# A sequence adapter kernel: another order of the beginning, high by high first

## The reference

```python
h = jnp.einsum('bsh,bhk->bsk', hidden_states, W_down[role]) + b_down[role][:, None, :]   # 1024 -> 512
h = jax.nn.gelu(h, approximate=False)
u = jnp.einsum('bsk,bkh->bsh', h, W_up[role]) + b_up[role][:, None, :]                   # 512 -> 1024
y = hidden_states + u
mean = jnp.mean(y, axis=-1, keepdims=True)
var = jnp.mean(jnp.square(y - mean), axis=-1, keepdims=True)
yn = (y - mean) * jax.lax.rsqrt(var + LN_EPS)
return yn * gamma[role][:, None, :] + beta[role][:, None, :]
```

## Time and profile before

| | us |
|---|---|
| median of 3 runs | 1417.29 (1417.27 to 1417.34) |
| the profiled execution | 1416.96 |
| its span | 1415.2 |
| PE busy | 1401.1 (99%) |
| DVE busy | 1204.8 (85%) |
| ACT busy | 776.8 (55%) |
| GpSimd busy | 201.0 (14%) |
| moved by DMA | 283.49 MB, 200 GB/s in the mean |

### The profile page before, as it was taken

One profiled execution on the slowest core, in us unless ns is written; L12 is line 12 of the kernel. 1 busy time (PEld: TensorE's weight loads), 2 busy tenths in 40 slices (PEclk: granted clock), 3 DMA queues, 4 the chain that ended last, 5 costly groups with the idle time before them and its releaser, 6 DMA issues.

```text
span 1415.2 us, 29331 instructions
## 1 busy us (share of the span) xinstructions
PE 1401.1 (99%) x6175; PEld 1158.2 (82%) x6176; DVE 1204.8 (85%) x1458; ACT 776.8 (55%) x2047; POOL 201.0 (14%) x300
## 2 busy tenths in 40 slices
PE   8999999999999999999999999999999999999997
PEld 6888888888888888888888888888888888888886
DVE  8798988888888888888888899988888888888887
ACT  5555555555555555555555555555555555555555
POOL 4376311100000000000000377311100000000000
PEclk9999999999999999999999999999999999999999
DMA  8677777766566666665666778777765666656654
GB/s 230 183 225 241 215 212 200 211 195 198 184 195 199 194 184 196 200 192 184 194 200 193 213 227 234 222 198 201 218 199 185 196 200 190 185 194 199 192 186 149
DMA packets 208868, 283.49 MB, mean 200 GB/s; under 512 B 25791, under 2 KB 155584, under 8 KB 208846
## 3 DMA queue, kind: packets, MB, share of 16 engines
q1 hardware_dynamic: 201438, 269.34, 61.4%
q0 software_dynamic: 5888, 12.07, 4.6%
q10 hardware_dynamic: 1520, 1.84, 0.4%
HBM read 183.27 MB, written 99.88 MB: 200 GB/s over the span
## 4 chain that ended last, share of the span: by engine, by line
PE 98%; DVE 1%; DMA 1%; issue 0%; ACT 0%; DVEq 0%; ACTq 0%
PE p_up L1120 16%; PE p_up L1118 16%; PE p_up L1119 16%; PE p_down L1118 16%; PE p_down L1120 16%; PE p_down L1119 16%; DMA row<-in_L_cond_W_down 0%; DMA x_quad<-in_x 0%; DVE row L1038 0%; PE p_hT L1114 0%; DVE row L866 0%; DMA w_raw<-in_itok_B 0%; DVE x_quad L820 0%; DVE wd_lo L758 0%; DVE x_quad L1024 0%
## 5 line engine op out<-in xcount | busy, mean ns | idle before, releaser
L1118 PE MATMUL p_down<-wd_hi,xT_hi 128*128 x1012 | 393.9, 389 | 0.7 <-DVE xT_lo L782 0.4
L1120 PE MATMUL p_down<-wd_hi,xT_lo 128*128 x1012 | 393.7, 389 | 0.0
L1119 PE MATMUL p_down<-wd_lo,xT_hi 128*128 x1012 | 393.7, 389 | 0.0
L1118 PE MATMUL p_up<-wu_hi,hT_hi 128*128 x1008 | 392.3, 389 | 0.0
L1120 PE MATMUL p_up<-wu_hi,hT_lo 128*128 x1008 | 392.1, 389 | 0.0
L1119 PE MATMUL p_up<-wu_lo,hT_hi 128*128 x1008 | 392.1, 389 | 0.0
L595 ACT ACTIVATE hT_hi<-p_hT 128x512 fp32r<-128x512 f32 x126 | 75.7, 601 | 381.5 <-DVE p_hT L800 378.9
L820 DVE SCALAR_TENSOR_TENSOR row<-p_up,row 128x1024 f32<-128x1024 f32 x126 | 154.2, 1224 | 126.3 <-PE p_up L1120 126.2
L581 ACT ACTIVATE xT_hi<-xT_raw 128x1024 fp32r<-128x1024 f32 x125 | 132.8, 1062 | 187.6 <-PE p_down L1120 185.6
L1118 PEld LDWEIGHTS p_down<-wd_hi,xT_hi 128*128 128x128 f32 x1012 | 189.6, 187 | 40.8 <-issue 1.4
L1119 PEld LDWEIGHTS p_down<-wd_lo,xT_hi 128*128 128x128 f32 x1012 | 190.3, 188 | 39.7
(11 more groups left out here) (174 smaller groups left out, 981.3 us busy)
## 6 DMA issues: line engine op xcount, KB each, us to landing
x_quad<-in_x SPq DMA_DIRECT2D x510, 128.0 KB, 3.4
row<-in_x SPq DMA_DIRECT2D x126, 512.0 KB, 4.0
out<-row SPq DMA_DIRECT2D x126, 512.0 KB, 2.7
h_dram<-h SPq DMA_DIRECT2D x125, 256.0 KB, 4.1
h_quad<-h_dram SPq DMA_DIRECT2D x498, 64.0 KB, 1.9
w_raw<-in_L_cond_W_down POOLq DMA_DIRECT2D x64, 64.0 KB, 3.2
w_raw<-in_L_cond_W_up POOLq DMA_DIRECT2D x64, 64.0 KB, 3.6
row<-in_L_cond_W_up SPq DMA_DIRECT2D x16, 128.0 KB, 3.6
```

Source lines behind the costliest of these rows:

```text
L1118: pe.matmul(dst, a_hi, w_hi, start=first, stop=False)
L1119: pe.matmul(dst, a_hi, w_lo, start=False, stop=False)
L1120: return pe.matmul(dst, a_lo, w_hi, start=False, stop=last)
```

## The change

- **Loads.** ACT issues only half of piece 1, rounds piece 0 first, and issues its two quarters of the first x after that. SP issues the other half of piece 1 behind its two quarters of the first x, then the second x, then pieces 2 and 3 whole. The numbers are read with one load instead of one for each x.
- **Parameter rows.** Their rounding moves from DVE to ACT, their subtraction behind `split_first(0)`.
- **DVE.** The selector is built ahead of the sort, the identity later. Both halves of the first x are transposed at once; `transpose_half(1, 1)` moves behind `split_first(2)` and `split_first(3)`.
- **ACT.** `round_first(1)` moves behind `round_half(0, 0)`, `copy_param(1)` behind `round_half(0, 1)`.
- **PE.** The matmuls on zeros go (with GpSimd's memset); five on W follow piece 0 and the two later ones go. `half_product` issues, for items 1 and 2, high by high of four chunks, high by low of four, then low by high; for item 0 it goes by pairs of chunks, each kind of matmul behind the wait for what it needs.

The number of product matmuls stays the same. The diff, with one line of context and without the list of semaphores:

```diff
@@ -307,10 +307,13 @@
 
+            number_reg = [sp.alloc_register(f"first_number{n}") for n in range(RING)]
             sp.wait_ge(first_known, 1)
-            for b, quads in ((0, range(0, NQ // 2)), (1, range(NQ))):
-                load_quads(sp, sp.value_load(first_numbers[0:1, b:b + 1], min_val=0, max_val=B - 1), b, quads)
-            load_first(sp, FD - 2, range(NQ // 2, NQ))
+            sp.load(number_reg, first_numbers[0:1, 0:RING])
+            load_quads(sp, sp.snap(number_reg[0], min_val=0, max_val=B - 1), 0, range(0, NQ // 2))
+            load_first(sp, 1, range(NQ // 2, NQ))
+            load_quads(sp, sp.snap(number_reg[1], min_val=0, max_val=B - 1), 1)
+            load_first(sp, FD - 2)
             load_first(sp, FD - 1)
@@ -396,7 +399,6 @@
             pool.memset(opener[:, 0:2], 0.0).then_inc(pieces_split, 1)
-            pool.memset(xT_lo[:, 0:HALF, :].bitcast(F32), 0.0).then_inc(zeros_ready, 1)
 
@@ -468,7 +470,7 @@
-            pool.wait_ge(ident_ready, 1)
+            pool.wait_ge(ident_ready, 2)
@@ -548,14 +550,20 @@
             load_first(act, 0, range(1, NQ))
-            load_first(act, 1)
-            act.wait_ge(first_known, 1)
-            load_quads(act, act.value_load(first_numbers[0:1, 0:1], min_val=0, max_val=B - 1), 0, range(NQ // 2, NQ))
+            load_first(act, 1, range(0, NQ // 2))
 
...
                 act.activation(hi, buf, ACT.Copy).then_inc(first_hi, 1)
+
+            round_first(0)
+            number_reg = [act.alloc_register(f"first_number{n}") for n in range(RING)]
+            act.wait_ge(first_known, 1)
+            act.load(number_reg, first_numbers[0:1, 0:RING])
+            load_quads(act, act.snap(number_reg[0], min_val=0, max_val=B - 1), 0, range(NQ // 2, NQ))
+            act.wait_ge(param_rows_loaded, 16 * 8)
+            act.activation(rows, rows_raw, ACT.Copy).then_inc(param_rows_hi, 1)
 
@@ -671,16 +679,14 @@
 
-            round_first(0)
             act.wait_ge(order_in_psum, 1)
             act.activation(table[0:1, NUMBER:NUMBER + B], p_up[0][0:1, 2 * B:3 * B], ACT.Copy).then_inc(numbers_ready, 1)
+            round_half(0, 0)
             round_first(1)
-            round_half(0, 0)
-            load_first(act, FD - 2, range(0, NQ // 2))
             copy_param(2, p_up[1][:, :], BETA, H, beta_loaded)
-            copy_param(1, p_hT[:, :], BD, K, bias_loaded)
             round_half(1, 0)
             round_half(0, 1)
+            copy_param(1, p_hT[:, :], BD, K, bias_loaded)
             round_first(2)
@@ -739,18 +745,17 @@
 
-            dve.wait_ge(key_spread, 1)
-            chain(dve.tensor_copy(key_col[:, :], p_up[0][:, B:B + 1]))
-            chain(dve.tensor_scalar(onehot, p_up[0][:, 0:B], key_col[:, :], None, ALU.is_gt, ALU.add, accum_out=rank[:, :]))
-            dve.tensor_scalar(onehot, index_row, rank[:, :], None, ALU.is_equal).then_inc(order_ready, 1)
-
             dve.tensor_scalar(row_of_col[:, 0:1].bitcast(I32), index_col[:, :], BLK - 1, None, ALU.bitwise_and).then_inc(row_known, 1)
...
                               ALU.is_equal).then_inc(ident_ready, 1)
-            dve.tensor_scalar(ident, index_row, number_col[:, :], None, ALU.is_equal).then_inc(ident_ready, 1)
+
+            dve.wait_ge(key_spread, 1)
+            chain(dve.tensor_copy(key_col[:, :], p_up[0][:, B:B + 1]))
+            chain(dve.tensor_scalar(onehot, p_up[0][:, 0:B], key_col[:, :], None, ALU.is_gt, ALU.add, accum_out=rank[:, :]))
+            dve.tensor_scalar(onehot, index_row, rank[:, :], None, ALU.is_equal).then_inc(order_ready, 1)
 
@@ -776,8 +781,6 @@
-                if (b, half) == (0, 0):
-                    dve.wait_ge(zeros_used, 1)
@@ -941,11 +944,6 @@
             params_at, when_loaded = [], []
-            dve.wait_ge(param_rows_loaded, 16 * 8)
-            dve.tensor_copy(rows, rows_raw).then_inc(param_rows_hi, 1)
-            dve.wait_ge(param_rows_hi, 1)
-            dve.tensor_tensor(rows[LOW:PAIRED, :], rows_raw[LOW:PAIRED, :], rows[LOW:PAIRED, :].bitcast(F32),
-                              ALU.subtract).then_inc(param_rows_split, 1)
             split_first(0)
@@ -953,17 +951,21 @@
                 when_loaded.append(dve.snap(slot_reg[b], min_val=0, max_val=1) * 16 + 16)
+            dve.wait_ge(param_rows_hi, 1)
+            dve.tensor_tensor(rows[LOW:PAIRED, :], rows_raw[LOW:PAIRED, :], rows[LOW:PAIRED, :].bitcast(F32),
+                              ALU.subtract).then_inc(param_rows_split, 1)
             transpose_half(0, 0)
+            transpose_half(0, 1)
+            subtract_half(0, 0)
+            dve.tensor_scalar(ident, index_row, number_col[:, :], None, ALU.is_equal).then_inc(ident_ready, 1)
             split_chunk(1, 0, chunk_split)
-            subtract_half(0, 0)
+            transpose_half(1, 0)
             split_chunk(1, 1, first_split)
-            transpose_half(1, 0)
-            transpose_half(0, 1)
             subtract_half(1, 0)
             subtract_half(0, 1)
-            transpose_half(1, 1)
             split_first(2)
             split_first(3)
+            transpose_half(1, 1)
             subtract_half(1, 1)
@@ -1084,13 +1086,9 @@
 
-            pe.wait_ge(zeros_ready, 1)
-            for _ in range(2):
-                mm = pe.matmul(p_down[:, :], xT_lo[:, 0, :], xT_lo[:, 0:HALF, :], start=True, stop=True)
-            mm.then_inc(zeros_used, 1)
             pe.wait_ge(first_hi, 1)
-            keep_clock(2)
-            pe.wait_ge(ident_ready, 2)
+            keep_clock(5)
+            pe.wait_ge(ident_ready, 1)
             pe.wait_ge(param_rows_split, 1)
@@ -1100,15 +1098,13 @@
             spread(p_up[0][:, 512:H], 6).then_inc(params_spread, 1)
-            keep_clock(1)
-            pe.wait_ge(half_hi, 1)
-            keep_clock(1)
 
...
                 else:
+                    pe.wait_ge(ident_ready, 2)
                     pe.wait_ge(bias_loaded, 16)
@@ -1157,37 +1153,67 @@
                 hi, lo = half_x(b, half)
-                for c in range(half * HALF, half * HALF + HALF):
-                    if (b, c) == (0, FC // K):
-                        pe.wait_ge(chunk_split, 1)
-                    elif (b, c) == (0, FC // K + 1):
-                        pe.wait_ge(first_split, 2)
-                    elif b == 0 and c % (FC // K) == 0:
-                        pe.wait_ge(first_split, c // (FC // K) + 1)
-                    mm = product(dst, hi[:, c % HALF, :], lo[:, c % HALF, :], cols(wd_hi, at + c * K, K),
-                                 cols(wd_lo, at + c * K, K), c == 0, c == HC - 1)
+                first, last = half * HALF, half * HALF + HALF - 1
+
+                def hi_by_hi(c):
+                    pe.matmul(dst, hi[:, c % HALF, :], cols(wd_hi, at + c * K, K), start=c == 0, stop=False)
+
+                def hi_by_lo(c, stop=False):
+                    return pe.matmul(dst, hi[:, c % HALF, :], cols(wd_lo, at + c * K, K), start=False, stop=stop)
+
+                def lo_by_hi(c, stop=False):
+                    return pe.matmul(dst, lo[:, c % HALF, :], cols(wd_hi, at + c * K, K), start=False, stop=stop)
+
+                chunks = range(first, last + 1)
+                x_hi, x_lo = (half_hi, half_lo) if half == 0 else (x_hi_ready, x_lo_ready)
+                pe.wait_ge(x_hi, b + 1)
+                if b > 0:
+                    for c in chunks:
+                        hi_by_hi(c)
+                    for c in chunks:
+                        hi_by_lo(c)
+                    pe.wait_ge(x_lo, b + 1)
+                    for c in chunks:
+                        mm = lo_by_hi(c, c == HC - 1)
+                    return mm
+                early, rest = chunks[0:2], chunks[2:4]
+                piece = first // 2
+                pe.wait_ge(first_hi, piece + 1)
+                for c in early:
+                    hi_by_hi(c)
+                pe.wait_ge(first_split, piece + 1)
+                for c in early:
+                    hi_by_lo(c)
+                pe.wait_ge(x_lo, 1)
+                for c in early:
+                    lo_by_hi(c)
+                pe.wait_ge(first_hi, piece + 2)
+                for c in rest:
+                    hi_by_hi(c)
+                for c in rest:
+                    lo_by_hi(c)
+                if half == 0:
+                    pe.wait_ge(chunk_split, 1)
+                    hi_by_lo(rest[0])
+                pe.wait_ge(first_split, piece + 2)
+                for c in rest[1 - half:]:
+                    mm = hi_by_lo(c, c == HC - 1)
                 return mm
...
             pe.wait_ge(pieces_split, when_split[0])
-            pe.wait_ge(half_lo, 1)
             half_product(0, 0, p_down[:, :], weights_at[0]).then_inc(half_down, 1)
             pe.wait_ge(pieces_split, when_split[1])
-            pe.wait_ge(half_lo, 2)
             pe.wait_ge(beta_loaded, 16)
             half_product(1, 0, other, weights_at[1]).then_inc(half_down, 1)
-            pe.wait_ge(x_lo_ready, 1)
```

(5 more changed lines are left out.)

## The result

The changed kernel takes 1419.15 us (median of 22 runs, 1418.84 to 1420.05) against 1417.36 for the kernel before (22 runs, 1417.13 to 1418.14): 1.79 us more, ratio 1.0012 with a 95% interval of 1.0007 to 1.0018. The forecast was 1418.7 (1417.5 to 1420.1), 1.4 more. The span of the profiled execution is 1417.3 us instead of 1415.2.

A forecast was written before the change was run, and what follows sets the result against it. The time was taken as fixed by when PE reaches the first h's transposes (23.75 us before). Terms -0.3, -0.1 and +1.85 gave +1.45: 1418.4 for the profiled execution, 1418.7 for the median, range 1417.5 to 1420.1.

The forecast's parts named there:

- main term: DVE transposes x1's second half behind W3's low part, delaying ACT's list; transposes of the first h at 25.2, +1.45 us.
- The tail: From the end of W3's low part to the transposes of the first h: 5.9 us, with no load in it.
- W3 lands at 17.0: Last quarter of W_down's fourth piece, issued by SP at about 12.8, lands at 17.0 us (15.6 to 17.8).
- x0 is there at 10.3: First x, its last quarters issued by ACT at 6.6 and 7.1, landed at 10.3 us (9.9 to 10.7) instead of 9.76.
- +1.45: Sum for the profiled execution: -0.3 start, -0.1 second start, +1.85 new idle and slower restart at 23.6 us.
- The rival of a light queue (b): Loads: with fewer in flight each lands after 2.8 us, W3 at 15.6; +0.95, 1418.2 us; chance 0.13.
- the estimate of 2.3 us: Load of one quarter: 2.0 us plus bytes over 436 GB/s; by it W3 lands at 15.1, sum +0.4 us.
- PE's own gain: PE's products before the first h's transposes: 0.2 to 0.5 us gained alone, covered by idleness from 23.6 to 25.2.
- Slack of at least 1.0: Behind the first h's transposes: inputs ready at least 1.0 us before PE needs them, so the shift is carried whole.
- Rival (a): A gain: earlier start and no stall at h, 1416.8 us; chance 0.09.
- Rival (c): PE's clock falls to 1.2 GHz at the start or the 23.6 us idle: 1420.1 to 1421.5 us; chance 0.05.
- Rival (d): Loads so late that matmul order never matters; W3 at 18.5 or later drives all: 1420.3 us; chance 0.05.

The follow-up runs named there:

- Experiment 2: Changed kernel with only DVE's transpose of the second x's second half back ahead of the low parts of the third and fourth W pieces: 1418.31 us.
- experiment 3: Changed kernel with ACT's copies of gamma and the up bias moved ahead of the rounding of the second x's second half: 1418.87 us.
- 11: Changed kernel with one more 1.0 us copy on ACT, and eight matmuls on W filling PE's idle ahead of the first h's transposes: 1420.13 us.
- Experiment 4: Changed kernel with PE's order of matmuls in the halves put back to that of the kernel before: 1419.41 us.
- 9: Kernel before with the new order of matmuls alone, and without the clock matmul behind the first half of x: 1417.70 us.
- Experiment 10: Changed kernel with one more 1.0 us copy on ACT behind the rounding of the second x's second half: 1421.71 us.
- experiment 7: Changed kernel with the old sharing of the loads and the second x's second half transposed ahead of the third and fourth pieces' low parts: 1418.12 us.
- experiment 5: Changed kernel with the loads of W pieces 1 and 2 shared as in the kernel before: 1418.83 us.
- 6: Changed kernel with the old sharing of the loads and three matmuls on W between the spreads and the first product: 1419.11 us.
- 12: Changed kernel with old load sharing, old place of the transpose, filled start, and ACT issuing its first x quarters before rounding piece 0: 1417.51 us.

## Why the prediction was right, point by point

**The place: right.** The forecast said that the time hangs on PE's arrival at the transposes of the first h, that x1's second transpose behind the low parts of pieces 3 and 4 is the main term, and that its tail is two copies, x2's half, bias and GELU. The chain of waits after shows just that. Experiment 2 removes the term (0.9), 3 fits the 0.35 of the exact list of ACT and DVE and rules out 1.35, and 11 shows that a copy put on it comes out at the end.

**The tail: right.** 5.9 us were worked out from the end of the fourth piece's low part to the transposes; it took 5.67 (20.06 to 25.73).

**The loads: right in kind, too small in size.** "W3 lands at 17.0" was 17.7, "x0 is there at 10.3" was 11.2, W3's low part ended at 20.06 and not at 19.3. These 0.76 us, less 0.23 by which the tail was shorter, are the whole difference between +1.45 and +1.98 in the profiled executions. The term that was mis-sized is the landing of W3's last quarter. The sum had 4.2 us for it (issued at 12.8, landed at 17.0), because it took the bytes to be moved by 15.8 to 16.2 with a fast stretch like the 304 GB/s of the earlier trace rows, and 1.2 us more to the landing. It was issued at 12.54 and took 5.17, after 259 GB/s in that stretch.

A second price was too low, that of ACT's x quarters: 3.2 us, from the rows of a kernel in which they left together with SP's. Now they took 3.8 and 4.4, with SP issuing two quarters of W1 from 6.26 and the second x from 7.35 beside them. It came close to setting the time too: with the late x, ACT was free for W3 at 17.4, not at 16.75. The Trainium skill, DMA: Bandwidth & Descriptors, Issuing engines are not separate DMA queues, says that transfers from both engines run interleaved on the same 16 DMA engines and that a second issuer only saves sequencer time; the trace agrees so far as ACT's second quarter, issued at 6.7 us, took 4.4 us beside SP's.

The rival of a light queue (b), with 2.8 us for each load, is out: the last quarter took 5.2. So is, as a price for these loads, the estimate of 2.3 us that the prediction worked out from the fit in the Trainium skill (DMA: Bandwidth & Descriptors, Anatomy of one DMA), which is for transfers issued by GpSimd.

**PE's own gain is covered: right, by another number.** Idle 1.22 and not 1.6, since the first product came at 12.75 and not at 11.85, with the late x. Experiment 4 shows that the matmul order hardly matters while the idle stretch is there (0.2 us in the median). Of the two signs of being wrong that the prediction named together, a first product later than 12.2 and a stall before the second half of x0, only the first came.

**"Slack of at least 1.0" behind the transposes** holds in the changed kernel (no wait there), but not as a bound for a mended one: in experiment 2 the x of item 3 lands late, PE waits at 36.79, and 0.9 us are lost from the transposes on. The prediction gave some 0.5 for a missing cover. I had named the W_up loads and x2 as level with before, and they were issued on time; what was missing is that a load issued on time can land 2 us later. By 24.2 us the changed kernel has moved 5.08 MB and the kernel before 5.47, so the bytes issued ahead of it were still in the way; that this is the reason is read from these sums, not tested by itself.

**Rival (a), a gain,** needed no stall at h. Even with the new matmuls alone (9) it isn't there.

**Rival (c), the clock: not in the changed kernel, but my reason against it was bad.** The 5 us without a fall at the end of the kernel were read as a bound. Experiment 10 has a fall behind 2.34 us of idleness, 4 within 2.48, 7 and 11 behind 1.78 and 1.79, while 1.22 in the changed kernel did nothing. The price was well sized: 1.4 us (between the medians of the two groups of experiment 10) to 1.6 (between 10 and 11), against the 1.4 to 2.8 given. The Trainium skill, TensorE: Matmul & The Clock Gate, What's actually happening, says that the slow level is the default, released by activity, and that the point of the change varies between executions of one kernel; the runs agree with the second as far as times tell (five executions of seven lie at 1421.7 to 1422.0, two 1.4 lower; one of the five was profiled).

**Rival (d)** had the loads late enough to rule all else; they were 0.7 late, not 1.5.

## What to carry to other kernels

Where PE is full nearly everywhere, look for the one wait ahead of the full stretch and list every instruction that stands behind it on each queue: a transpose moved behind two subtractions carried 5.7 us of copies and activations with it. Don't price a load by its own median in another kernel: look at what the other queues have issued before and beside it. An issue 0.6 us later landed 1.9 us later in one pair of executions, and one 0.45 earlier landed later too in another. DMA time left idle at the start was not made up here. And fill idle stretches of PE with matmuls before comparing variants, or the clock will decide some executions.

## What the runs showed of the hardware

- The granted clock fell to 0.50 (1.2 GHz) at the end of, or behind, an idle stretch of PE of 1.78 us (experiment 7), 1.79 (11) and 2.34 (10), for 3.4 us each time, and within one of 2.48 us (4), for 6.8 us. It stayed at 1.00 after idle stretches of up to 1.31 us (experiment 3, before the first product), and after the last matmul of the kernel before for 5 us. By its times the same kernel (10) fell in five executions and not in two.
- In experiment 10 the fall came 0.5 us after PE had begun to work again (27.4 against 26.89), in 4 while it was still idle (12.8 against 13.50).
- Two x quarters issued by ACT at 5.84 us and 0.5 later landed after 2.7 and 3.1 us (experiment 5), at 6.41 and 6.9 after 3.5 and 4.4 (6), and at 5.39 and 5.9 after 3.2 and 4.1 (12), with SP issuing a quarter each 0.5 us meanwhile.
